# A bias row for two tiles on one engine, and two one-hots in one comparison, in a graph network's edge loop

## The chip, the cores and the metric

The kernel runs on one NeuronCore of a Trainium2 chip. The metric is the device time of one execution in microseconds (us); the times are medians of several runs. The profile and the trace come from one more, profiled execution. "TensorE" is PE in the rows, its weight loads are PEld, VectorE is DVE, ScalarE is ACT, GpSimd is POOL and SyncE is SP.

## The reference, cut to what matters

There are 1250 nodes of 512 features and 20000 edges, sorted by their destination. Two graph layers run one after the other. The first (layer norm, relu, sum over in-edges, two matrix products with batch norm) is not touched. The second is:

```python
h = mish(concat([x[src], x[dst], edge_attr], -1) @ W1 + b1)   # first edge layer, 20000 x 512
messages = mish(h @ W2 + b2)                                  # second edge layer, 20000 x 512
agg = segment_sum(messages, dst, num_segments=1250)
u = mish(concat([x, agg], -1) @ W3 + b3)
out = u @ W4 + b4                                             # then x + out, layer norm, residual
```

with `mish(x) = x * tanh(softplus(x))`. `b2` is one row of 512 values, the same for every edge.

## The kernel before, in words

The products `x @ W1` for the source and the destination part are made once per node and stored as two tables. The edges are cut into tiles of 128, two tiles to a **step** (numbered s, from 0 to 78; step 78 has one tile). Each step gathers its rows of both tables (GpSimd's indirect DMAs), and then five kinds of work run, each engine in its own written order and all tied by semaphores:

- **z1** (TensorE, `z1`, L1099 and L1106): transposes the gathered rows into PSUM and adds the edge attributes' product. It waits for `h_full` of step s-1, since there is one pair of banks `Z1`.
- **mish 1** (ScalarE, `exp1`, `sq1`, `log1`, `inv1`, L1422 to L1434), then VectorE: `full1` (L2098, tile `h_full`, in two halves), `hi1` (L2108, the rounded part of h) and `lo1` (L2112, the rest of h).
- **z2** (TensorE, `z2`): for each of the two tiles k = 0 and 1 of the step, h times W2 in three terms of four matmuls: `h_hi` by both parts of W2 (L1124, L1125), then `h_lo` by one part (L1129). Each is a 128x512 matmul. The result of tile k of step s stands in bank `2 * (s % 2) + k` of `Z2`.
- **mish 2** (ScalarE, `exp2` to `inv2`, L1446 to L1458), then VectorE: `message` (L2123), `hi2` (L2133), `lo2` (L2137).
- **segment** (TensorE, L1149): four matmuls of the one-hot destinations with the messages. VectorE makes the one-hots (`hots1`, L1645, by comparing a row of numbers with each edge's destination). Two steps, an odd and the even one after it, gather in one bank; VectorE adds the bank to the nodes (`add_group`, L1656, two instructions) in every even step of its own order, after it has waited for `seg_done`.

The orders are these. TensorE in step s: z1 of s; z2 of s-2, tile 1; segment of s-4; z2 of s-1, tile 0. VectorE in step s: full1 of s; hi2 of s-3; hi1 of s; lo2 of s-3; message of s-2; one-hots of s-2; b2 row for step s; lo1 of s; in even steps the sums of s-3. ScalarE in step s: exp1, sq1, log1 of s; exp2 of s-2; inv1 of s; sq2; (in odd steps the b2 copy for s-1); log2; inv2 of s-2. A second part of the sums for destinations outside the usual window stands in a branch that is entered only where it is needed.

The bias b2 has to stand in a Z2 bank before the matmuls that accumulate there. From step 2 on three ways are used. For tile 0 VectorE copies the row (`b2_first_tile`, L2127), in every step. For tile 1 of even steps ScalarE copies it (`b2_second_tile`, L1461). For tile 1 of odd steps TensorE makes it by a matmul of ones with the row (L1122), as it does for all four tiles of steps 0 and 1. TensorE waits for a semaphore ahead of a z2 whose row was copied:

```python
if after(s, 2) and k == 0:
    pe.wait_ge(b2_first, s - 1)
elif after(s, 2) and j == 0:
    pe.wait_ge(b2_second, s)
else:
    pe.matmul(at, ONES_R[:, :], B2_R[:, :], start=True, stop=False, ...)
```

Here j is s % 2 and `after(s, 2)` is true from step 2 on. VectorE may write the row only when `message` of step s-2, which reads the same banks, is done.

Of the kernel before, what the change touches and what calls it, by code (L numbers as in the profile page):

```python
# [17 lines left out]
ALU = mybir.AluOpType  # L18
# [8 lines left out]
P = 128  # L27
NODES, DIM, HID0, EDGE_DIM = 1250, 512, 1024, 64
# [95 lines left out]
def gnn_kernel(nc, x, src_cols, dst_cols, dst_rows, edge_attr_t, eps, cols, rows, w01, w02,  # L124
               w1, w2, w3, w4, out):
    ctx = ExitStack()
    with ctx:
# [3 lines left out]
        def sb(name, shape, dt=F32, at=None):  # L131
            size = 2 if dt in (F16, I16) else 4
            for n in shape[1:]:
                size *= n
            if at is None:
                at = place[0]
                place[0] += size + (-size) % 32
            return nc.alloc_sbuf_tensor_at(name, shape, dt, offset=at), at + size + (-size) % 32
# [27 lines left out]
        REL_G, _ = sb("dst_in_group", [P, TILES])  # L166
# [5 lines left out]
        ONEHOT, _ = sb("onehot", [P, 2, 2, P], F32R)  # L172
# [16 lines left out]
        IOTA, _ = sb("iota", [P, NP])  # L189
# [4 lines left out]
        B2_ROW, _ = sb("b2_row", [P, 1, DIM], at=place[0] - 4 * 4 * PW)  # L194
# [132 lines left out]
        def h_high(s, j):  # L327
            return EARLY_HI[:, :, :] if early(s, 1) else H_HI[:, j, :, :]

        def h_low(s, j):  # L330
            return EARLY_LO[:, :, :] if early(s, 1) else H_LO[:, j, :, :]
# [27 lines left out]
        Z1, SEG, Z2 = BANKS[:, 0:2, :], BANKS[:, 2:4, :], BANKS[:, 4:8, :]  # L359
# [13 lines left out]
        def sem(name):  # L373
            return ctx.enter_context(nc.semaphore(name))
# [20 lines left out]
        hot_ready, seg_done, agg_done = sem("hot_ready"), sem("seg_done"), sem("agg_done")  # L395
# [16 lines left out]
        z1_done, a_exp, a_sq, a_ln, a_r, h_hi, h_lo = (sem(n) for n in  # L412
            ("z1_done", "a_exp", "a_sq", "a_ln", "a_r", "h_hi", "h_lo"))
        h_full = [sem(f"h_full_{h}") for h in range(2)]
        z2_done, b2_in, b2_first, b2_second = (sem(n) for n in ("z2_done", "b2_row_in", "b2_in_first_tile", "b2_in_second_tile"))
        b_exp, b_sq, b_ln, b_r, msg_full, msg_hi, msg_lo = (sem(n) for n in
            ("b_exp", "b_sq", "b_ln", "b_r", "msg_full", "msg_hi", "msg_lo"))
        u_bias, u_exp, u_cut, u_sq, u_ln, u_r, u_ready = (sem(n) for n in
# [13 lines left out]
        def live(s):  # L432

            return not isinstance(s, int) or 0 <= s < EDGE_PAIRS

        def tiles(s):

            return min(2, EDGE_TILES - 2 * s) if isinstance(s, int) else 2
# [7 lines left out]
        def after(s, first):  # L446

            return not isinstance(s, int) or s >= first
# [387 lines left out]
        def _(pe):  # L836
# [273 lines left out]
            def z2(s, j, k):  # L1110

                at, e = Z2[:, 2 * j + k, :], slice(k * P, (k + 1) * P)
                if k == 0:
                    if not after(s, 2):
                        pe.wait_ge(up_moved, BLOCKS * KD)
                    pe.wait_ge(h_hi, s + 1)
                if after(s, 2) and k == 0:
                    pe.wait_ge(b2_first, s - 1)
                elif after(s, 2) and j == 0:
                    pe.wait_ge(b2_second, s)  # L1120
                else:
                    pe.matmul(at, ONES_R[:, :], B2_R[:, :], start=True, stop=False, skip_group_check=True)  # L1122
                for c in range(KD):
                    pe.matmul(at, h_high(s, j)[:, c, e], W2_LO[:, c, :], start=False, stop=False, skip_group_check=True)  # L1124
                    pe.matmul(at, h_high(s, j)[:, c, e], W2_HI[:, c, :], start=False, stop=False, skip_group_check=True)  # L1125
                if k == 0:
                    pe.wait_ge(h_lo, s + 1)
                for c in range(KD):
                    mm = pe.matmul(at, h_low(s, j)[:, c, e], W2_HI[:, c, :], start=False, stop=(c == KD - 1), skip_group_check=True)  # L1129
                if k == tiles(s) - 1:  # L1130
                    mm.then_inc(z2_done, 1)
# [43 lines left out]
            for b in range(BLOCKS):  # L1175
                for o in range(KD):
                    n = KD * b + o
# [5 lines left out]
                    if n in Z1_BEHIND:  # L1183
                        s = Z1_BEHIND.index(n)
# [58 lines left out]
        def _(act):  # L1243
# [174 lines left out]
            def exp1(s):  # L1418
                act.wait_ge(z1_done, s + 1)
                if after(s, 1):  # L1420
                    act.wait_ge(h_full[1], s)
                nc.scalar.activation(z1_work(s)[:, :, 0:P * tiles(s)], Z1v[:, :, 0:P * tiles(s)], ACT.Exp).then_inc(a_exp, 1)  # L1422
# [34 lines left out]
                act.wait_ge(b_ln, s + 1)  # L1457
                nc.scalar.activation(z2_work(s), z2_work(s), ACT.Exp, scale=-1.0).then_inc(b_r, 1)  # L1458

            def b2_second_tile(s, j):  # L1460
                nc.scalar.copy(Z2[:, 2 * j + 1, :], B2_ROW[:, 0, :]).then_inc(b2_second, 2)  # L1461

            def edge_step(s, j):

                if live(s):
                    exp1(s)
                    sq1(s)
                    log1(s)
                if live(s - 2):
                    exp2(s - 2, j)  # L1470
                if live(s):
                    inv1(s)
                if live(s - 2):
                    sq2(s - 2)
                if j == 1 and after(s, 3) and live(s - 1) and tiles(s - 1) == 2:
                    b2_second_tile(s - 1, 1 - j)
                if live(s - 2):
                    log2(s - 2)
                if live(s - 2):
                    inv2(s - 2)  # L1480

            act.wait_ge(q_stored, TABLE_STORED)
            for b in range(BLOCKS):
                for o in range(KD):
                    n = KD * b + o
# [4 lines left out]
                    for s, first in enumerate(Z1_BEHIND):  # L1490
# [5 lines left out]
                            log1(s)  # L1496
                        if n == first + 3:
                            inv1(s)
            act.wait_ge(b2_in, 16)
            for s in range(2, 4):  # L1500
                edge_step(s, s % 2)
            with act.Fori(2, LAST - 1) as i:
# [66 lines left out]
        def _(dve):  # L1569
# [61 lines left out]
            def load_range(n, row):  # L1631

                dve.load(range_regs[n][:R_USED], range_words(row, R_LOW, R_USED))
# [8 lines left out]
            def make_hots(hots, rel, tile, past=0):  # L1642

                for j, at in enumerate(hots):
                    ins = nc.vector.tensor_scalar(at, IOTA[:, bass.ds(past * P, P)], rel[:, bass.ds(tile + j, 1)], None, ALU.is_equal)  # L1645
                return ins
# [467 lines left out]

            def hots1(s, j):

                make_hots([ONEHOT[:, j, k, :] for k in range(2)], REL_G, 2 * s).then_inc(hot_ready, 1)

            def message(s, j):
                dve.wait_ge(b_r, s + 1)  # L2120
# [1 line left out]
                    dve.wait_ge(msg_lo, s)  # L2122
                nc.vector.scalar_tensor_tensor(MSG[:, :, :], EB[:, :, :], -0.5, z2_out(s, j), ALU.add, ALU.mult).then_inc(msg_full, 1)  # L2123

            def b2_first_tile(s, j):
                dve.wait_ge(msg_full, s - 1)
                nc.vector.tensor_copy(Z2[:, 2 * j, :], B2_ROW[:, 0, :]).then_inc(b2_first, 1)  # L2127

            def hi2(s):
                dve.wait_ge(msg_full, s + 1)  # L2130
# [27 lines left out]
            def edge_step(s, j, i):  # L2158

                if live(s):  # L2160
                    for h in range(2):
                        full1(s, h)
                if live(s - 3):
                    hi2(s - 3)
                if live(s):
                    hi1(s, j)
                if live(s - 3):
                    lo2(s - 3)
                if live(s - 2):
                    message(s - 2, j)  # L2170
                if live(s - 2):
                    hots1(s - 2, j)
                    if live(s):
                        b2_first_tile(s, j)
                if live(s):
                    lo1(s, j)
                if live(s - 3):
                    sums1(s - 3, i - 2 + j, j == 0)
                if live(s - 2) and j == 0:
                    load_range(0, i - 1)  # L2180
# [159 lines left out]
```

## Time and profile before

| | before |
|---|---|
| time, median of 3 runs (lowest to highest) | 1098.36 us (1097.97 to 1099.22) |
| the profiled execution: its own time | 1101.45 us |
| its span in the trace | 1099.6 us |
| TensorE busy, matmuls / weight loads | 1041.4 us (95%) / 875.5 us (80%) |
| VectorE busy | 869.0 us (79%) |
| ScalarE busy | 886.9 us (81%) |
| GpSimd busy | 716.9 us (65%) |
| granted TensorE clock over the span, mean | 0.977 of full |
| chain that ended last, by engine | TensorE 86%, VectorE 7%, ScalarE 3% |

The span is the profiled stretch from the first to the last instruction. The edge loop takes it from about 370 us to 1032 us. "Busy" counts an engine's instructions and not its register, wait or branch instructions; weight loads run beside matmuls. A matmul of 128x512 shows 0.39 us in its row while the next one starts 0.23 us later, because they are pipelined.

### The profile page before, as it was taken

The page shows a single profiled execution, that of the slowest core. Times are in us where ns is not written, and L with a number is a line of the kernel's source. Part 1 is how long each engine was busy: PE and PEld are TensorE (multiplying, and loading weights), DVE is VectorE, ACT ScalarE, POOL GpSimd, SP SyncE. Part 2 cuts the span into 40 slices and gives each one's busy share as a digit, 9 for nine tenths or more (in the row PEclk, how much of TensorE's full clock was granted, in tenths as well). Part 3 has the DMA queues.
Part 4 walks back from the last instruction along what each step waited for, and adds up shares of the span by engine and source line. Part 5 has one row for each costly group of instructions (what it writes and reads, how often), then busy time and mean ns, then how long its engine had stood idle before and what let it go on. Part 6 is the DMA issues. An engine that isn't in the chain of part 4 may idle for free.

```text
span 1099.6 us, 18587 instructions
## 1 busy us (share of the span) xinstructions
PE 1041.4 (95%) x5641; PEld 875.5 (80%) x5642; DVE 869.0 (79%) x1504; ACT 886.9 (81%) x1081; POOL 716.9 (65%) x622
## 2 busy tenths in 40 slices
PE   3568999999999999999999999999999999999997
PEld 1126889999789888888888888888888888888796
DVE  7898536634525389999999999999999999999786
ACT  6985845523613699999999999999999999999584
POOL 6875448643255487777777777777777777760217
PEclk8769999999999999999999999999999999999999
DMA  3004972674165386676666667666666666661002
GB/s 105 8 1 113 177 230 76 228 252 142 59 229 115 78 198 162 158 165 140 137 140 147 135 140 143 145 138 140 145 139 137 145 143 137 142 127 39 1 1 94
DMA packets 82914, 141.63 MB, mean 129 GB/s; under 512 B 11115, under 2 KB 39020, under 8 KB 82742
## 3 DMA queue, kind: packets, MB, share of 16 engines
q0 software_dynamic: 38048, 87.58, 39.2%
q1 hardware_dynamic: 44822, 53.52, 15.1%
q8 instruction: 21, 0.34, 0.1%
q14 instruction: 23, 0.19, 0.1%
HBM read 115.42 MB, written 20.39 MB: 124 GB/s over the span
## 4 chain that ended last, share of the span: by engine, by line
PE 86%; DVE 7%; ACT 3%; issue 2%; POOL 1%; DMA 1%; DVEq 1%; POOLq 0%; ACTq 0%
PE banks L1124 13%; PE banks L1125 13%; PE banks L1129 13%; PE banks L1023 9%; PE banks L1106 7%; PE banks L1149 7%; PE banks L1099 6%; PE banks L1066 5%; PE banks L941 4%; PE banks L1087 4%; PE banks L1210 2%; DVE edge_counts L1790 2%; DVE key_onehot L1729 1%; PE banks L996 1%; PE banks L871 1%
## 5 line engine op out<-in xcount | busy, mean ns | idle before, releaser
L774 POOL DMA_INDIRECT gather_pq<-q_table,dst x157 | 323.4, 2060 | 57.1 <-issue 47.5
L766 POOL DMA_INDIRECT gather_pq<-p_table,src x157 | 174.7, 1113 | 119.5 <-PE banks L1106 68.5
L1124 PE MATMUL banks<-w_lo,h_hi 128*128 128x512 f32 x620 | 241.9, 390 | 0.0
L1125 PE MATMUL banks<-w_hi,h_hi 128*128 128x512 f32 x620 | 241.7, 390 | 0.0
L1129 PE MATMUL banks<-w_hi,h_lo 128*128 128x512 f32 x620 | 166.0, 390 | 0.0
L1129 PEld LDWEIGHTS banks<-w_hi,h_lo 128*128 128x128 f32 x620 | 116.4, 188 | 24.3
L1125 PEld LDWEIGHTS banks<-w_hi,h_hi 128*128 128x128 f32 x620 | 116.4, 188 | 23.7
L1124 PEld LDWEIGHTS banks<-w_lo,h_hi 128*128 128x128 f32 x620 | 116.4, 188 | 23.3 <-issue 0.6
L2098 DVE SCALAR_TENSOR_TENSOR h_full<-mish_work,banks 128x512 f32<-128x512 f32 (+1 forms) x154 | 98.4, 680 | 44.5 <-ACT mish_work L1434 41.4
L2123 DVE SCALAR_TENSOR_TENSOR message<-mish_work,banks 128x1024 f32<-128x1024 f32 x78 | 95.3, 1222 | 8.4 <-ACT mish_work L1458 0.3
L1099 PE MATMUL banks<-ident,gather_pq 128*128 128x128 f32 x628 | 96.5, 275 | 0.6 <-DVE h_full L2098 0.3
L1106 PE MATMUL banks<-edge_attr_parts,we_hi 128*128 128x256 f32 (+1 forms) x316 | 94.6, 322 | 0.0
L2137 DVE TENSOR_TENSOR message_lo<-message,message_hi 128x1024 fp32r<-128x1024 f32 x78 | 94.3, 1209 | 0.1
L2112 DVE TENSOR_TENSOR h_lo<-h_full,h_hi 128x1024 fp32r<-128x1024 f32 (+1 forms) x77 | 93.1, 1209 | 0.0
L1099 PEld LDWEIGHTS banks<-ident,gather_pq 128*128 128x128 f32 x628 | 72.0, 140 | 17.3 <-DVE h_full L2098 11.0
L1458 ACT ACTIVATE mish_work<-mish_work 128x1024 f32<-128x1024 f32 (+1 forms) x79 | 83.5, 1057 | 2.5
L1454 ACT ACTIVATE mish_work<-mish_work 128x1024 f32<-128x1024 f32 (+1 forms) x79 | 83.2, 1054 | 1.3
L1422 ACT ACTIVATE mish_work<-banks 128x1024 f32<-128x1024 f32 (+1 forms) x77 | 78.6, 1021 | 6.0 <-PE banks L1106 5.2
L1426 ACT ACTIVATE mish_work<-mish_work 128x1024 f32<-128x1024 f32 (+1 forms) x77 | 81.3, 1056 | 2.5
L1430 ACT ACTIVATE mish_work<-mish_work 128x1024 f32<-128x1024 f32 (+1 forms) x77 | 81.3, 1056 | 2.4
L1450 ACT ACTIVATE mish_work<-mish_work 128x1024 f32<-128x1024 f32 (+1 forms) x79 | 82.4, 1043 | 0.1
L1106 PE MATMUL banks<-edge_attr_parts,we_lo 128*128 128x256 f32 (+1 forms) x316 | 81.6, 280 | 0.0
(270 smaller groups left out, 2623.4 us busy)
## 6 DMA issues: line engine op xcount, KB each, us to landing
edge_attr<-in_edge_attr_t SPq DMA_DIRECT2D x20, 256.0 KB, 2.9
attr_high<-edge_attr_hi SPq DMA_DIRECT2D x40, 128.0 KB, 2.1
attr_low<-edge_attr_lo SPq DMA_DIRECT2D x40, 128.0 KB, 1.8
edge_attr_parts<-attr_high SPq DMA_DIRECT2D x79, 64.0 KB, 2.5
edge_attr_parts<-attr_low SPq DMA_DIRECT2D x79, 64.0 KB, 2.4
x_nodes<-h_hi POOLq DMA_DIRECT2D x10, 256.0 KB, 14.9
x_nodes<-h_lo POOLq DMA_DIRECT2D x10, 256.0 KB, 7.8
p_table<-p_stage SPq DMA_DIRECT2D x10, 256.0 KB, 2.0
```

Of the source, the lines that this page charges most:

```text
L766: nc.gpsimd.indirect_dma_start(GP[:, 2 * j + k, :], None, p_tab[:, :], bass.IndirectOffsetOnAxis(ap=SRC[:, 2 * s + k:2 * s + k + 1], axis= ...
L774: nc.gpsimd.indirect_dma_start(GP[:, 2 * j + k, :], None, q_tab[:, :], bass.IndirectOffsetOnAxis(ap=DST[:, 2 * s + k:2 * s + k + 1], axis= ...
L1023: mm = pe.matmul(bank, weights[w][:, k, o * P:(o + 1) * P], acts[a](k)[:, nodes], start=(k == 0 and n == 0), stop=(k == kn - 1 and n == 2) ...
L1099: pe.matmul(Z1v[:, c, k * P:(k + 1) * P], GP[:, 2 * slot + k, c * P:(c + 1) * P], IDENT[:, :], is_transpose=True, skip_group_check=True, s ...
L1106: mm = pe.matmul(Z1v[:, c, 0:P * tiles(s)], w[:, c * P:(c + 1) * P], AT_R[:, slot, 0:P * tiles(s)], skip_group_check=True, start=False, st ...
L1124: pe.matmul(at, h_high(s, j)[:, c, e], W2_LO[:, c, :], start=False, stop=False, skip_group_check=True)
L1125: pe.matmul(at, h_high(s, j)[:, c, e], W2_HI[:, c, :], start=False, stop=False, skip_group_check=True)
L1129: mm = pe.matmul(at, h_low(s, j)[:, c, e], W2_HI[:, c, :], start=False, stop=(c == KD - 1), skip_group_check=True)
L2098: nc.vector.scalar_tensor_tensor(h_full_of(s)[:, at[0], at[1]], z1_work(s)[:, at[0], at[1]], -0.5, Z1v[:, at[0], at[1]], ALU.add, ALU.mult ...
L2112: nc.vector.tensor_tensor(h_low(s, j)[:, :, 0:P * tiles(s)], h_full_of(s)[:, :, 0:P * tiles(s)], h_high(s, j)[:, :, 0:P * tiles(s)].bitcas ...
L2123: nc.vector.scalar_tensor_tensor(MSG[:, :, :], EB[:, :, :], -0.5, z2_out(s, j), ALU.add, ALU.mult).then_inc(msg_full, 1)
L2137: nc.vector.tensor_tensor(MSG_LO[:, :, :], MSG[:, :, :], MSG_HI[:, :, :].bitcast(F32), ALU.subtract).then_inc(msg_lo, 1)
```

## The change

VectorE copies the b2 row into both tiles' banks in every step from 2 on, in one instruction of 1024 columns. ScalarE's copy and its semaphore are gone, and so is TensorE's bias matmul from step 2 on; TensorE waits for the one new semaphore ahead of tile 0 of each step. The two one-hots of a step are made by one tensor-tensor comparison of 256 columns, whose operands are the row of numbers, repeated for both tiles, and each tile's column of destinations, repeated 128 times.

```diff
-                if after(s, 2) and k == 0:
-                    pe.wait_ge(b2_first, s - 1)
-                elif after(s, 2) and j == 0:
-                    pe.wait_ge(b2_second, s)
+                if after(s, 2):
+                    if k == 0:
+                        pe.wait_ge(b2_seeded, s - 1)
                 else:
                     pe.matmul(at, ONES_R[:, :], B2_R[:, :], start=True, stop=False, skip_group_check=True)
...
-            def b2_second_tile(s, j):
-                nc.scalar.copy(Z2[:, 2 * j + 1, :], B2_ROW[:, 0, :]).then_inc(b2_second, 2)
...
-                if j == 1 and after(s, 3) and live(s - 1) and tiles(s - 1) == 2:
-                    b2_second_tile(s - 1, 1 - j)
...
-                make_hots([ONEHOT[:, j, k, :] for k in range(2)], REL_G, 2 * s).then_inc(hot_ready, 1)
+                wide = [P, 2, P]
+                nc.vector.tensor_tensor(ONEHOT[:, j, :, :], IOTA[:, 0:P].rearrange("p (o k) -> p o k", o=1).broadcast_to(wide),
+                                        REL_G[:, bass.ds(2 * s, 2)].rearrange("p (t o) -> p t o", o=1).broadcast_to(wide),
+                                        ALU.is_equal).then_inc(hot_ready, 1)
...
-            def b2_first_tile(s, j):
+            def b2_both_tiles(s, j):
                 dve.wait_ge(msg_full, s - 1)
-                nc.vector.tensor_copy(Z2[:, 2 * j, :], B2_ROW[:, 0, :]).then_inc(b2_first, 1)
+                nc.vector.tensor_copy(Z2[:, 2 * j:2 * j + 2, :], B2_ROW[:, :, :].broadcast_to([P, 2, DIM])).then_inc(b2_seeded, 1)
```

`make_hots` issued one tensor-scalar comparison of 128 columns for each tile. ScalarE's wait for the row's load, ahead of its loop, is also taken out.

## Rows read from the trace of the kernel before

**Rows 1.** Busy time by engine, 400 to 1000 us, granted clock, DMA share, GB/s.
```profile
400.00:1000.00 600.00, 600.00 (x3185) 507.38 (x3185) 550.30 (x790) 591.21 (x611) 455.51 (x281) 1.00 0.67 141
```

**Rows 2.** Instructions of L1122, L1461, L2127: duration min/median/max, first and last start.
```profile
L1122 PE MATMUL banks<-b_parts,ones x42: 389/397/497, 369.7 to 1016.5; 128*128 128x512 f32 x42
...
L1461 ACT COPY banks<-b_row x38: 584/586/592, 388.8 to 1008.0; 128x512 f32<-128x512 f32 x38
...
L2127 DVE COPY banks<-b_row x77: 683/685/691, 384.6 to 1019.2; 128x512 f32<-128x512 f32 x77
```

**Rows 3.** Timeline of VectorE: start us, duration us, instruction [idle before it].
```profile
606.04 1.28 DVE L2098 SCALAR_TENSOR_TENSOR h_full<-mish_work,banks 128x512 f32<-128x512 f32 x2
...
611.29 0.68 DVE L2127 COPY banks<-b_row 128x512 f32<-128x512 f32 x1
611.89 1.21 DVE L2112 TENSOR_TENSOR h_lo<-h_full,h_hi 128x1024 fp32r<-128x1024 f32 x1
613.96 1.28 DVE L2098 SCALAR_TENSOR_TENSOR h_full<-mish_work,banks 128x512 f32<-128x512 f32 x2 [0.85 <-ACT mish_work L1434]
...
618.83 0.48 DVE L1645 TENSOR_SCALAR onehot<-iota,dst_in_group 128x128 fp32r<-128x128 f32 x2
619.22 0.69 DVE L2127 COPY banks<-b_row 128x512 f32<-128x512 f32 x1
619.81 1.22 DVE L2112 TENSOR_TENSOR h_lo<-h_full,h_hi 128x1024 fp32r<-128x1024 f32 x1
621.29 0.75 DVE L1656 SCALAR_TENSOR_TENSOR agg_nodes<-banks,from_low,agg_nodes 128x512 f32 x1 [0.26 <-issue]
621.96 0.74 DVE L1656 SCALAR_TENSOR_TENSOR agg_nodes<-banks,below_low,agg_nodes 128x512 f32 x1
622.78 1.28 DVE L2098 SCALAR_TENSOR_TENSOR h_full<-mish_work,banks 128x512 f32<-128x512 f32 x2
```

**Rows 4.** TensorE and its weight loads: timelines; the L1122 row from the chain.
```profile
606.78 0.31 PEld L1099 LDWEIGHTS banks<-ident,gather_pq 128*128 128x128 f32 x3 [0.28 <-DVE h_full L2098]
...
612.13 0.19 PEld L1124 LDWEIGHTS banks<-w_lo,h_hi 128*128 128x128 f32 x1
...
612.58 0.39 PE L1125 MATMUL banks<-w_hi,h_hi 128*128 128x512 f32 x1
...
617.06 0.23 PE banks L1122
...
620.55 0.39 PE L1149 MATMUL banks<-message_lo,onehot 128*128 128x512 f32 x1
```

**Rows 5.** Timelines of VectorE, the weight loads and TensorE near the loop's end.
```profile
1012.82 0.69 DVE L2127 COPY banks<-b_row 128x512 f32<-128x512 f32 x1
...
1013.62 0.19 PEld L1124 LDWEIGHTS banks<-w_lo,h_hi 128*128 128x128 f32 x1 [0.41 <-issue]
...
1013.96 0.40 PE L1125 MATMUL banks<-w_hi,h_hi 128*128 128x512 f32 x1
```

**Rows 6.** Timelines of TensorE and VectorE where the sums come first.
```profile
402.81 0.39 PE L1149 MATMUL banks<-message_lo,onehot 128*128 128x512 f32 x1
...
402.35 1.21 DVE L2112 TENSOR_TENSOR h_lo<-h_full,h_hi 128x1024 fp32r<-128x1024 f32 x1
403.56 0.75 DVE L1656 SCALAR_TENSOR_TENSOR agg_nodes<-banks,from_low,agg_nodes 128x512 f32 x1
```

**Rows 7.** Groups by line and shape: count | busy us, mean ns | idle before.
```profile
L2123 DVE SCALAR_TENSOR_TENSOR message<-mish_work,banks 128x1024 f32<-128x1024 f32 x78 | 95.3, 1222 | 8.4 <-ACT mish_work L1458 0.3
...
L2133 DVE CAST message_hi<-message 128x1024 fp32r<-128x1024 f32 x78 | 53.9, 690 | 0.4 <-DVE message L2123 0.4
...
L2021 DVE TENSOR_TENSOR x_nodes<-x_nodes,banks 128x256 f32<-128x256 f32 x4 | 1.6, 409 | 1.3 <-PE banks L996 1.3
...
L1981 DVE SCALAR_TENSOR_TENSOR dst_in_group<-ranges,dst_f 128x160 f32<-128x160 f32 x1 | 0.3, 314 | 0.0
...
L1719 DVE SCALAR_TENSOR_TENSOR key<-src_parts,dst_from_lowest 128x160 f32<-128x160 f32 x1 | 0.3, 313 | 0.0
```

More of the change, by code:

```diff
@@ L414, in gnn_kernel @@
         h_full = [sem(f"h_full_{h}") for h in range(2)]
-        z2_done, b2_in, b2_first, b2_second = (sem(n) for n in ("z2_done", "b2_row_in", "b2_in_first_tile", "b2_in_second_tile"))
+        z2_done, b2_in, b2_seeded = (sem(n) for n in ("z2_done", "b2_row_in", "b2_in_both_tiles"))
         b_exp, b_sq, b_ln, b_r, msg_full, msg_hi, msg_lo = (sem(n) for n in
@@ L1474, in edge_step @@
                     sq2(s - 2)
-                if j == 1 and after(s, 3) and live(s - 1) and tiles(s - 1) == 2:
-                    b2_second_tile(s - 1, 1 - j)
-                if live(s - 2):
                     log2(s - 2)
@@ L1498, in _ @@
                             inv1(s)
-            act.wait_ge(b2_in, 16)
             for s in range(2, 4):
@@ L2173, in edge_step @@
                     if live(s):
-                        b2_first_tile(s, j)
+                        b2_both_tiles(s, j)
                 if live(s):
```

## The prediction, made before the changed kernel ran

> **What bounds the kernel now.** The engines' busy time by stage comes first. Between 400 and 1000 us the kernel runs its edge loop; TensorE is busy in every microsecond, ScalarE in 591 of 600 and VectorE in 550, at the full clock [rows 1]. With three engines this full, shares do not say which waits decide, so the timelines of one period come next. A period is two steps (an even pair of tiles, then an odd one). ScalarE's copy runs once in each, 38 times from 388.8 to 1008.0, which makes (1008.0 - 388.8) / 37 = 16.74 us a period [rows 2].
>
> In the period from 606.04 VectorE begins h_full of an odd step at 606.04 and of the next even step at 613.96, after 0.85 us idle for ScalarE's last exponential, and the next odd one at 622.78 [rows 3]. So there is slack of 0.85 us in the odd step's VectorE work. In the even step the only idle is 0.26 us ahead of the node sums (L1656) at 621.29. The profile puts it down to "issue". I read it as a wait for TensorE: the last of the four segment matmuls starts at 620.55 and takes 0.39 [rows 4], so it ends at 620.94 and the sum starts 0.35 later. In the first period that ends in sums the last segment matmul ends at 402.81 + 0.39 = 403.20 and the sum starts at 403.56, 0.36 later, while h_lo before it started 1.21 earlier, against 1.48 at 619.81 [rows 3, 6]. The distance to TensorE is the same and the distance to VectorE's own work is not.
>
> That gives two closed loops.
> - **Loop P:** h_full odd (606.04), TensorE's z1, z2, segment, z2 of the odd pair (first weight load 612.13), z1, the bias matmul, z2, segment (ends 620.94), VectorE's sums, h_full odd (622.78). Length 16.74. TensorE hardly stops in it: the load for z1 at 606.78, which waits for h_full, is the one row in a period with a wait on it [rows 4].
> - **Loop V:** h_full odd, z1, ScalarE's four steps, h_full even: 7.92 us; then VectorE's own chain from h_full even to h_full odd, 8.82 us as measured. Without the wait for the segment it would be shorter: h_lo at 619.81 and, since an instruction here starts about 0.08 before the end of the one ahead, the first sum 1.14 later at 620.95, 0.34 sooner. And the sums' last 0.82 (621.96 to 622.78) would be 0.67, as between the two sums, because the registers would have been loaded meanwhile. So 8.82 - 0.34 - 0.15 = 8.33, and loop V has 0.49 us to spare.
>
> **The change, part by part.**
> *TensorE's bias matmul goes* in odd steps from 3 on. Of 42 such matmuls [rows 2] the four of steps 0 and 1 stay, 38 go. Each holds the chain for 0.23 us [rows 4]. It lies in loop P, between z1 and the segment. Taken alone: -0.23 x 37 = -8.5 us.
> *ScalarE's copy goes*, 38 times 0.59 us. I cost that at nothing: exp of z1 waits for TensorE and h_full even waits for the exponential of that same chain, in which the copy (after the second square) does not stand. VectorE's message waits for ScalarE's last inverse, whose half a microsecond of lead only grows. Its semaphore falls away too.
> *VectorE's row becomes two rows.* The 512-column copy takes 0.69 us [rows 3]. A 1024-column instruction with a PSUM operand takes 1.22 (L2123, mean 1222 ns), so +0.53 for each of 77 copies. The bound below: the 1024-column cast between SBUF tiles takes 0.69 [rows 7], which would make the addition nothing. I take 1.22, since the present copy needs 0.69 for 512 columns: it runs at the rate of the former, with the same fixed part.
> *Two one-hots become one comparison.* Now 0.39 us from the first to the copy (618.83 to 619.22) [rows 3]. One tensor-tensor over 256 columns takes 0.41 (L2021), less 0.08 of overlap, 0.33 [rows 7]: -0.06. Its bounds: 0.27 more if the repeated operands went at half rate, or nothing gained.
> Sum for VectorE: +0.47 us a step, all ahead of h_lo and, for TensorE, ahead of z2.
>
> *The even step.* Its copy would end at 613.96 + 5.26 - 0.06 + 1.22 = 620.38. TensorE reaches that z2 at 620.78 less 0.23, so it waits for nothing. Loop V becomes 7.92 + 8.33 + 0.47 = 16.72: all slack used, no cost, and about 0.02 under today's period.
> *The odd step.* h_full even has 0.85 us of cover, 0.47 of which is used. But TensorE takes the odd z2 sooner here: the copy ends 606.04 + 5.25 - 0.06 + 1.22 = 612.45, after the 612.13 at which its first load starts now [rows 4]. The semaphore wait added here is on TensorE, and the whole of z2, the next z1, z2 and segment are queued behind it. What a late row costs is seen once in the trace, near the end: the copy at 1012.82 ends at 1013.51, the load starts at 1013.62 and the second matmul at 1013.96, 0.45 after the copy's end [rows 5]. So the second matmul would start at 612.90 instead of 612.58: +0.32 in loop P, against -0.23 from the bias matmul. Loop P: 16.74 - 0.23 + 0.32 = 16.83, and it is the longer one. h_lo, also 0.47 later (ends 613.57), is needed only after eight matmuls of 0.23, past 614.4, and stays covered.
>
> So a period grows by 0.08 us (0.02 less to 0.15 more, as the copy or the restart come out 0.05 to 0.1 other than taken). Over the 36 periods between the first sums and the end: +2.9 us. The first period with sums starts its sum when VectorE can, 1.21 after h_lo, so there VectorE's 0.47 shows by about 0.2. In the last three steps VectorE has no pause; three copies of 0.47 come to at most 1.4, less what ScalarE and TensorE hide; I take 0.8. Sum 2.9 + 0.2 + 0.8 = +3.9 us, bounds 0 and 7. On the profiled execution, 1101.45 us (span 1099.6, and 1.85 around it), that is 1105.3. The median shown, 1098.36, lies 3.09 below the profiled one; the same addition gives 1102.2.
>
> **A rule against the change.** The one-hots' second operand repeats one column's value 128 times. In the trace the add of the lowest rows (L1981) reads an operand whose every value is repeated four times, 160 elements, in 314 ns; L1719 reads 160 plain ones twice in 313 ns [rows 7]. Repeating costs nothing there. The Trainium skill ("Vector Engine (DVE) Microarchitecture Reference", section 5.2 on stream behaviour) says that a port streams at the full rate only where elements come in runs of at least two adjacent words, and gives 1.73 ns a column with one source hopping; by that figure the comparison would take an estimated 0.18 us more than I count. The trace speaks against it, in runs of four only; it is the first rival.
>
> **Rivals.**
> *A, slow comparison.* The operand repeated 128 times goes at up to half rate, at most 0.27 us more. The row in PSUM comes later by as much and loop P with it. At two thirds of that bound, 0.18 x 36 = +6.5 on top: 1108.7. For it: no row repeats one value so long. Against: L1981. Chance 0.10.
> *B, faster.* The copy of both rows runs at the pitch of the SBUF casts, 0.69 for 1024 columns. Then the row is in time for TensorE, VectorE's chain is 0.06 shorter, and what is left is the bias matmul's -0.23 a period: 37 x 0.23 = 8.5, 1089.9. It decides once the copy takes under about 0.9, the length at which the load at 612.13 is no longer late. For it: SBUF casts of this size. Against: the copy's own 0.69 for 512 columns. Beside it, the Trainium skill ("VectorE: DVE Perf Modes", "Why PSUM operands drop a tier") holds fp32 with a PSUM operand to one element a cycle; by it B would not occur, and this trace's copy row agrees. Chance 0.13, part of it for a gain that these rows do not show me.
> *C, no slack in the even step.* If the 0.26 ahead of the sums is what the profile calls it, issue time after h_lo [rows 3], VectorE's 0.47 goes into every period in full: 36 x 0.47 + 1 = +18, 1116. Against: the constant 0.35 behind the segment [rows 3, 4, 6]. Chance 0.05.
>
> **How the numbers follow.** The forecast has 0.72, own range 1098 to 1105.5. A run tells 0.2% (2.2 us) from no change, so "same" ends at 1100.6. Of the 0.72 I give 0.22 to the part below that (a period that changes by 0.03 or less) and 0.50 above. Slower: 0.50 + 0.10 + 0.05 = 0.65; same 0.22; faster 0.13. The range 1097.5 to 1108.8 leaves out B, C and little else.
>
> **What would show it.** Period of VectorE's h_full rows: 16.83 (forecast), 16.51 (B), 17.0 (A), 17.2 (C). The copy row 128x1024 at 1.22; the comparison at 0.41. The idle before L1656 gone in even steps, that before h_full even down from 0.85 to about 0.4. On TensorE a new wait once a period at the first load of the odd z2, L1124, put down to the copy; were it missing, loop P is wrong. No L1461 rows, 4 of L1122. ScalarE's idle grows by about 0.6 us a period.

## The result, and the profile after

The changed kernel takes 1103.62 us in the median of its runs (1102.5 to 1105.68), the kernel before 1098.36; the ratio is 1.0046, with a 95% interval of 1.0037 to 1.0054. So it is slower, by 5.1 us (4.1 to 5.9). The prediction said 1102.2, +3.9.

First the page of the kernel after: its span, each engine's busy time, its share and the count of instructions. Behind it, from the same kernel, the busy time by engine from 400 to 1000 us, in the order of [rows 1].

```profile
span 1100.9 us, 18306 instructions
...
PE 1046.8 (95%) x5603; PEld 866.0 (79%) x5604; DVE 901.6 (82%) x1427; ACT 873.9 (79%) x1043; POOL 692.4 (63%) x622
```

```profile
400.00:1000.00 600.00, 597.45 (x3129) 494.02 (x3128) 577.11 (x712) 574.66 (x570) 427.61 (x279) 1.00 0.68 140
```

Against [rows 1] VectorE is busy 26.8 us more and ScalarE 16.5 us less. TensorE, which was busy in every microsecond, now is not for 2.55 us, and it finished 56 matmuls fewer in the same 600 us. About 36 of them are the bias matmuls of some 36 periods; the other 20 it did not get to: it waits.

Next, lines of the kernel after as instructions: duration min/median/max in ns, first and last start in us. They answer to [rows 2]; the last is the first sum of each pair (L1656 before).

```profile
L1121 PE MATMUL banks<-b_parts,ones x4: 389/396/497, 365.8 to 378.7; 128*128 128x512 f32 x4
...
L2122 DVE COPY banks<-b_row x77: 1218/1220/1226, 380.6 to 1020.5; 128x1024 f32<-128x1024 f32 x77
...
L2110 DVE TENSOR_TENSOR onehot<-iota,dst_in_group x77: 416/418/421, 380.3 to 1020.1; 128x256 fp32r<-128x256 f32 x77
...
L1648 DVE SCALAR_TENSOR_TENSOR agg_nodes<-banks,from_low,agg_nodes x40: 742/746/752, 399.9 to 1032.4; 128x512 f32 x40
```

Four bias matmuls are left and no copy by ScalarE. From the first sum to the last it takes 632.5 us here. The same line of the kernel before reads so:

```profile
L1656 DVE SCALAR_TENSOR_TENSOR agg_nodes<-banks,from_low,agg_nodes x40: 743/751/753, 403.6 to 1031.1; 128x512 f32 x40
```

That is 627.5, so the loop became 5.0 us longer. Taken from each odd step's `h_full`, the mean of 36 periods went from 16.736 to 16.868 us (405.07 to 1007.57 before, 401.18 to 1008.43 after): 36 x 0.132 = +4.75. From the last of them to the end it is 92.07 before and 92.47 after, +0.40. The sum, +5.15, agrees with the measured 5.1.

The spans differ by only 1.3 us, because the loop of the profiled execution of before began 3.9 us later. That is no effect of the change: in the profiled runs below, the same point lies anywhere from 400.9 to 405.1, in kernels with the old and with the new loop.

The timeline of VectorE in one period of the kernel after (start us, duration us, instruction [idle before it]), to be read beside [rows 3]:

```profile
603.72 1.28 DVE L2090 SCALAR_TENSOR_TENSOR h_full<-mish_work,banks 128x512 f32<-128x512 f32 x2
...
608.60 0.42 DVE L2110 TENSOR_TENSOR onehot<-iota,dst_in_group 128x256 fp32r<-128x256 f32 x1
608.93 1.22 DVE L2122 COPY banks<-b_row 128x1024 f32<-128x1024 f32 x1
610.06 1.22 DVE L2104 TENSOR_TENSOR h_lo<-h_full,h_hi 128x1024 fp32r<-128x1024 f32 x1
611.65 1.28 DVE L2090 SCALAR_TENSOR_TENSOR h_full<-mish_work,banks 128x512 f32<-128x512 f32 x2 [0.37 <-ACT mish_work L1433]
...
617.98 1.21 DVE L2104 TENSOR_TENSOR h_lo<-h_full,h_hi 128x1024 fp32r<-128x1024 f32 x1
619.11 0.74 DVE L1648 SCALAR_TENSOR_TENSOR agg_nodes<-banks,from_low,agg_nodes 128x512 f32 x1
619.77 0.74 DVE L1648 SCALAR_TENSOR_TENSOR agg_nodes<-banks,below_low,agg_nodes 128x512 f32 x1
620.60 1.28 DVE L2090 SCALAR_TENSOR_TENSOR h_full<-mish_work,banks 128x512 f32<-128x512 f32 x2
```

The idle ahead of the sums (0.26 before) is gone, and the one ahead of the even `h_full` has shrunk from 0.85 to 0.37. TensorE at the odd step's row, in the kernel after, weight loads and matmuls:

```profile
610.27 0.19 PEld L1123 LDWEIGHTS banks<-w_lo,h_hi 128*128 128x128 f32 x1 [0.52 <-issue]
```

```profile
610.30 0.47 PE L1123 MATMUL banks<-w_lo,h_hi 128*128 128x512 f32 x1
610.61 0.40 PE L1124 MATMUL banks<-w_hi,h_hi 128*128 128x512 f32 x1
...
618.37 0.39 PE L1148 MATMUL banks<-message_lo,onehot 128*128 128x512 f32 x1
```

The row's copy ends at 608.93 + 1.22 = 610.15 and the load starts 0.12 later, after a pause that was not there before. The list of waits from 400 to 1000 us of the kernel after (us in total, times, longest) shows it once a period, under two names:

```profile
ACT mish_work L1421 <- PE banks L1106: 13.6, 36, 0.5
DVE h_full L2090 <- ACT mish_work L1433: 13.4, 36, 0.4
PEld banks L1123 <- issue: 10.3, 19, 0.6
PEld banks L1099 <- DVE h_full L2090: 10.0, 35, 0.4
PEld banks L1123 <- DVE banks L2122: 7.6, 17, 0.5
```

19 + 17 = 36. Both names stand for one wait, that for the copy. The distance from the copy's end to the load alternates from period to period, between 0.12, as above, and 0.05. ScalarE now waits for z1 once a period, which it did not before: it has lost its copy, and its work is no longer near the bound.

### The profile page after: what moved, and what is told of

Same layout as the page of the kernel before. It is cut to its first block and busy times, and to the rows that moved or that the text cites. A ratio compares the mean times of both kernels' runs of the same rounds, so it can differ in the third digit from the quotient of the medians.

```text
span 1100.9 us, 18306 instructions
## 1 busy us (share of the span) xinstructions
PE 1046.8 (95%) x5603; PEld 866.0 (79%) x5604; DVE 901.6 (82%) x1427; ACT 873.9 (79%) x1043; POOL 692.4 (63%) x622
## 5 line engine op out<-in xcount | busy, mean ns | idle before, releaser
L774 POOL DMA_INDIRECT gather_pq<-q_table,dst x157 | 297.7, 1896 | 57.4 <-issue 47.5
L1123 PE MATMUL banks<-w_lo,h_hi 128*128 128x512 f32 x620 | 246.2, 397 | 3.5 <-DVE banks L2122 1.9
L2122 DVE COPY banks<-b_row 128x1024 f32<-128x1024 f32 x77 | 94.0, 1221 | 0.0
```

What stands on the lines that cost most here:

```text
L774: nc.gpsimd.indirect_dma_start(GP[:, 2 * j + k, :], None, q_tab[:, :], bass.IndirectOffsetOnAxis(ap=DST[:, 2 * s + k:2 * s + k + 1], axis= ...
L2122: nc.vector.tensor_copy(Z2[:, 2 * j:2 * j + 2, :], B2_ROW[:, :, :].broadcast_to([P, 2, DIM])).then_inc(b2_seeded, 1)
```

## The experiments

The theory, **P**, is the prediction's: the loop through TensorE binds, and the odd row's late copy costs it more than the bias matmul gave back. The rivals are that VectorE's even step binds (C), that the comparison is the culprit (A), and that the matmul's removal was worth nothing. The ratio is always to the kernel before as timed on the same chip, so that kernel's median differs a little from one experiment to another; "period" is the mean from one odd step's `h_full` to the next in the profiled execution, over the same 36 periods in every kernel, 16.736 before and 16.868 after.

### One comparison alone

The kernel before, with nothing but the new comparison:

```diff
-                make_hots([ONEHOT[:, j, k, :] for k in range(2)], REL_G, 2 * s).then_inc(hot_ready, 1)
+                nc.vector.tensor_tensor(ONEHOT[:, j, :, :], ..., ..., ALU.is_equal).then_inc(hot_ready, 1)
```

> The kernel before with the one comparison alone. Theory P: VectorE is not in the binding loop ahead of the segment, so its 0.06 us a step goes into slack: ratio 1.000 (within 0.001). Rival V (VectorE's time counts in every step): 0.12 us a period, 4 us less, ratio 0.996.

1099.91 against 1100.08 us, ratio 1.0001 (0.999 to 1.0012), period 16.744. In even steps the comparison gains VectorE 0.05 us (the copy begins 5.21 instead of 5.26 after the even `h_full`). In odd steps it gains nothing here (5.28, and 5.27 before), because the cast of the messages, which stands ahead of it, takes over 0.73 us in 35 of the 36 odd steps, where 3 did before. The kernel gains nothing. With only about 0.06 a period left to gain, rival V would have come to an estimated ratio of 0.998, which the interval still leaves out. The rival A is out: the comparison costs no time.

### 0.3 us more on VectorE, in the even or in the odd step

A comparison of 184 columns, whose result nobody reads, is added to the kernel before. In the first kernel it stands behind `h_lo` in even steps, in the second ahead of the row's copy in odd ones:

```diff
+            def pad():
+                nc.vector.tensor_tensor(PAD[:, :], IOTA[:, 0:184], IOTA[:, 0:184], ALU.is_equal)
...
                     lo1(s, j)
+                    if live(s - 2) and j == 0:
+                        pad()
```

```diff
                     hots1(s - 2, j)
+                    if j == 1:
+                        pad()
                     if live(s):
                         b2_first_tile(s, j)
```

> The kernel before, with one more VectorE instruction (184 columns, about 0.26 us, its result unused) after h_lo in even steps, just ahead of the idle that the profile calls issue. Reading of the prediction: that idle is a wait for TensorE's segment, the even step has 0.49 us to spare, so nothing changes: period 16.74, ratio 1.000 (within 0.001). Rival C (the idle is issue time and VectorE's chain has no slack there): 37 x 0.26 = 9.6 us more, ratio 1.0088.

> The kernel before, with the same extra instruction (0.26 us) in odd steps, ahead of the copy of the row. Theory P: the row of odd steps, just in time before, comes 0.26 late; the second matmul of that z2 moves from 6.54 to 5.94 + 0.26 + 0.45 = 6.65 after h_full, so the period grows by 0.11 to 0.15: 4 to 5.5 us, ratio 1.0037 to 1.005. Rival (only idle of VectorE itself counts): the odd step has 0.85 us idle, so nothing changes, ratio 1.000.

Even: 1098.16 against 1100.08 us, ratio 0.9988 (0.9977 to 0.9999), period 16.742. VectorE's timeline in that kernel:

```profile
598.89 1.22 DVE L2113 TENSOR_TENSOR h_lo<-h_full,h_hi 128x1024 fp32r<-128x1024 f32 x1
600.03 0.34 DVE L2121 TENSOR_TENSOR pad<-iota 128x184 fp32r<-128x184 f32 x1
600.37 0.75 DVE L1657 SCALAR_TENSOR_TENSOR agg_nodes<-banks,from_low,agg_nodes 128x512 f32 x1
...
601.86 1.29 DVE L2099 SCALAR_TENSOR_TENSOR h_full<-mish_work,banks 128x512 f32<-128x512 f32 x2
```

The pad stands where the idle was, and the time did not rise (the interval ends just under 1.000, and the period is that of before). In TensorE's timeline the last segment matmul ends where it should for that:

```profile
599.63 0.39 PE L1150 MATMUL banks<-message_lo,onehot 128*128 128x512 f32 x1
```

599.63 + 0.39 = 600.02, and the sum follows 0.35 later as before. What the profile calls "issue" there is the wait for the segment. Rival C is out.

Odd: 1105.14 us, ratio 1.0048 (1.0031 to 1.0064), period 16.890. The same third of a microsecond, of which 0.26 goes by before the copy starts, put where VectorE itself still idles afterwards, costs 0.15 a period:

```profile
612.73 0.34 DVE L2121 TENSOR_TENSOR pad<-iota 128x184 fp32r<-128x184 f32 x1
612.99 0.69 DVE L2131 COPY banks<-b_row 128x512 f32<-128x512 f32 x1
...
615.37 1.29 DVE L2099 SCALAR_TENSOR_TENSOR h_full<-mish_work,banks 128x512 f32<-128x512 f32 x2 [0.56 <-ACT mish_work L1435]
```

VectorE still waits 0.56 us for ScalarE. What the pad delays is the row, and by it TensorE: its second matmul of the odd z2 comes 6.66 after the odd `h_full`, where it was 6.54 before. This is P's first half shown in the kernel before, with no second row and no missing matmul. The two pads are one instruction with one price; only the place differs.

### The bias matmul put back

The changed kernel, with TensorE's bias matmul kept for tile 1 of odd steps:

```diff
-                if after(s, 2):
-                    if k == 0:
-                        pe.wait_ge(b2_seeded, s - 1)
-                else:
+                if after(s, 2) and k == 0:
+                    pe.wait_ge(b2_seeded, s - 1)
+                elif not after(s, 2) or j == 1:
                     pe.matmul(at, ONES_R[:, :], B2_R[:, :], start=True, stop=False, ...)
```

> The changed kernel, but TensorE still makes the row of tile 1 in odd steps by its matmul (over VectorE's row). Theory P (the late row stands in TensorE's loop, and the removed matmul had paid for part of it in the same loop): the period of two steps goes from 16.87 to 16.87 + 0.23 = 17.10 us, 8.5 us above the changed kernel, ratio to the kernel before 1.0125. Rival V (in the changed kernel VectorE's own chain sets the period): the matmul lies off that chain, nothing changes against the changed kernel, ratio 1.0046.

1111.71 against 1099.07 us, ratio 1.0112 (1.0087 to 1.0137), period 17.073, +0.205 over the changed kernel. So the matmul was in the loop that binds and its removal is worth 36 x 0.205 = 7.4 us. The change as a whole lost 4.75 in the loop, so everything else in it cost some 12.

### The odd row sooner: three ways

P's own remedy is to bring the odd row in time. First, tile 0's row alone at the old place, and tile 1's behind `h_lo` (even steps as in the changed kernel):

```diff
+                if j == 1:
+                    nc.vector.tensor_copy(Z2[:, 2 * j, :], B2_ROW[:, 0, :]).then_inc(b2_seeded, 1)
+                    return
                 nc.vector.tensor_copy(Z2[:, 2 * j:2 * j + 2, :], B2_ROW[:, :, :].broadcast_to([P, 2, DIM])).then_inc(b2_seeded, 1)
...
                     lo1(s, j)
+                if j == 1 and after(s, 3) and live(s):
+                    b2_odd_second(s, j)
```

> The changed kernel, but in odd steps VectorE writes only tile 0's row at the old place and tile 1's row after h_lo, as a copy of its own (even steps write both at once). ScalarE's copy and TensorE's matmul stay out. Theory P: TensorE's wait for the row in odd steps is gone, its loop falls to 16.74 - 0.23 = 16.51, and VectorE's chain of 7.92 + 8.80 (to 8.85) is the longer one: period 16.72 to 16.77, ratio to before 0.999 to 1.002. Rival V (all of VectorE's added time counts): 0.07 more VectorE work a period than in the changed kernel, 16.94, ratio 1.007.

1102.12 us, ratio 1.0025 (1.0013 to 1.0038), period 16.797. TensorE's wait at the odd row is gone (second matmul 6.57 after the odd `h_full` in the mean, instead of 6.86). The loop through VectorE's even step now binds, as computed: it measures 8.79 from `h_full` even to odd in the median, and in about every second period 16.70 to 16.73 in all. Most of the others are 16.84 or longer, which was not expected; the last section comes back to it.

Second, the copy ahead of the comparison in odd steps:

```diff
                 if live(s - 2):
+                    if j == 1 and live(s):
+                        b2_both_tiles(s, j)
                     hots1(s - 2, j)
-                    if live(s):
+                    if j == 0 and live(s):
                         b2_both_tiles(s, j)
```

> The changed kernel, but in odd steps VectorE copies the row ahead of the comparison. The copy then waits only for message, so it starts about 0.15 us sooner (5.05 after h_full odd instead of 5.20). Theory P: the period falls by as much as the row comes sooner, 16.87 to 16.72, where VectorE's chain (7.92 + 8.80) takes over; period 16.72 to 16.80, ratio to before 1.000 to 1.003. Rival V: VectorE's work is the same, period 16.87, ratio 1.0046 or a little more.

1115.24 us, ratio 1.0125 (1.0097 to 1.0153), period 17.214: a plain miss of every theory. The row did come sooner (the copy ends 6.21 after the odd `h_full` instead of 6.43), and the kernel became slower.

Third, with TensorE's matmul still replaced but ScalarE's copy kept: the kernel before, with the one comparison, and VectorE's second copy only in odd steps, behind `h_lo`.

```diff
+                elif after(s, 2):
+                    pe.wait_ge(b2_odd, s - 1)
                 else:
                     pe.matmul(at, ONES_R[:, :], B2_R[:, :], start=True, stop=False, ...)
...
                     lo1(s, j)
+                if j == 1 and after(s, 3) and live(s):
+                    b2_odd_second(s, j)
```

> The kernel before, with ScalarE's copy for tile 1 of even steps and VectorE's 512-column copy for tile 0 as they were, the one comparison, and only TensorE's matmul replaced: VectorE copies tile 1's row of odd steps after h_lo. Theory P: TensorE's loop falls to 16.51, VectorE's even chain keeps its half microsecond of slack, and its odd step keeps 0.85 + 0.06 - 0.60 = 0.3; ScalarE, whose idle is about 0.14 a period before, becomes the bound at about 16.60: 37 x 0.14 = 5 us under the kernel before, ratio 0.9955. Rival V: VectorE has 0.48 us more work a period than before and the time rises, ratio above 1.005.

1092.88 us, ratio 0.9941 (0.9919 to 0.9962), period 16.580. This beats both kernels. VectorE's timeline of its odd step:

```profile
607.02 0.69 DVE L2132 COPY banks<-b_row 128x512 f32<-128x512 f32 x1
607.62 1.22 DVE L2114 TENSOR_TENSOR h_lo<-h_full,h_hi 128x1024 fp32r<-128x1024 f32 x1
608.75 0.69 DVE L2135 COPY banks<-b_row 128x512 f32<-128x512 f32 x1
609.69 0.69 DVE L2100 SCALAR_TENSOR_TENSOR h_full<-mish_work,banks 128x512 f32<-128x512 f32 x1 [0.25 <-ACT mish_work L1436]
```

The first row is where it was, the second fills the idle ahead of the even `h_full`, and 0.25 of that idle is left in this period (0.25 to 0.51 over the loop). The even step holds nothing new. So the gain of the matmul can be had; the changed kernel gave it back, with more, for a row in the odd step that is late and a row in the even step that ScalarE had been writing for nothing.

### Both rows with the two old comparisons

> The changed kernel with the two old comparisons, so the rows alone. Theory P: the row comes 0.05 us later than in the changed kernel, and the period grows by that: 16.92, 2 us above the changed kernel, ratio to before 1.0065. If only VectorE's chain counted (rival V), the same 0.05 stands in one chain of the even step: 16.92 as well; this run is for the size, that of one comparison's worth where the row is late.

The changed kernel, with `make_hots` as before. 1128.11 against 1100.08 us, ratio 1.0257 (1.0237 to 1.0277), period 17.545 (17.58 without the last two periods, the figure in the expectation below), where +0.05 on the changed kernel had been expected and it was +0.68. This is the second miss, and it shows in VectorE's and GpSimd's timelines of this kernel:

```profile
611.93 0.74 DVE L1648 SCALAR_TENSOR_TENSOR agg_nodes<-banks,from_low,agg_nodes 128x512 f32 x1
612.46 1.56 POOL L774 DMA_INDIRECT gather_pq<-q_table,dst  x1 [0.30 <-issue]
612.59 0.73 DVE L1648 SCALAR_TENSOR_TENSOR agg_nodes<-banks,below_low,agg_nodes 128x512 f32 x1
613.95 1.29 DVE L2090 SCALAR_TENSOR_TENSOR h_full<-mish_work,banks 128x512 f32<-128x512 f32 x2 [0.62 <-issue]
```

Between the second sum and `h_full` VectorE stands still for 0.62 us, and ScalarE has nothing to do with it. What stands in that place of VectorE's order is `load_range`: its sequencer loads three words from SBUF into registers, for the next sums. The line of that load (DVEq, VectorE's sequencer; min/median/max in ns), in the kernel before, in the changed one, in this one, and in the one with the row first:

```profile
L1633 DVEq TENSOR_LOAD <-tile_range x40: 744/750/769, 384.3 to 1029.7; - x40
```

```profile
L1625 DVEq TENSOR_LOAD <-tile_range x40: 744/750/757, 380.4 to 1031.2; - x40
```

```profile
L1625 DVEq TENSOR_LOAD <-tile_range x40: 745/1474/1591, 382.5 to 1057.7; - x40
```

```profile
L1625 DVEq TENSOR_LOAD <-tile_range x40: 745/1380/1583, 384.6 to 1047.7; - x40
```

The load takes 0.75 us in the first two and up to 1.59 in the others. In the kernel with the old comparisons each load of the loop that is long (33 of 35, 1.14 to 1.59 us) has one of GpSimd's gathers from the second table (L774) begin 0.14 to 0.17 us after its own start; above, the load starts at 612.29 and the gather at 612.46. With the row first it is 0.13 to 0.35 us in 34 of 35. In the kernels before and after, no gather begins in the load's first 0.5 us. This made a theory, **L**: a register load is stretched when a gather begins early in it, and VectorE's sums had been moved onto such a place. It was tried by moving the load.

### The register load moved

In these kernels `load_range` is issued in the odd step behind `h_lo`, where VectorE waits for ScalarE anyway:

```diff
                     lo1(s, j)
+                if live(s - 2) and j == 1:
+                    load_range(0, i - 1)
                 if live(s - 3):
                     sums1(s - 3, i - 2 + j, j == 0)
-                if live(s - 2) and j == 0:
+                if isinstance(s, int) and s == FINAL:
                     load_range(0, i - 1)
```

First with the two old comparisons:

> The run of the rows alone, whose period was 17.58 and not 16.92, with one move: VectorE's register load of the next group's ranges, which its sequencer makes behind the node sums of even steps, is issued in the odd step instead, behind h_lo. Theory L (the missed 0.66 us is that load, 1.48 long where a GpSimd gather of the second table begins inside it, and 0.75 elsewhere): the h_full of odd steps comes about 0.65 us after the second sum again, the period is 16.92 - 0.17 = 16.75 (to 16.85), ratio to before 1.000 to 1.006. Rival (the old pair of comparisons with the long copy costs it in another way): 17.4 or more, ratio above 1.02.

Then with the row first in odd steps:

> The run with the row ahead of the comparison in odd steps, with the same move of the load. Theory L with P: its load too was 1.44 long. Without it TensorE's loop is 16.87 - 0.22 (row sooner) - 0.17 (load) = 16.5 and VectorE's chain 7.92 + 8.80 = 16.72 is the bound: 16.70 to 16.80, ratio 0.999 to 1.003. Rival (the order of copy and comparison itself cost the time): stays near 17.2, ratio 1.0125.

The two come to 1104.12 (ratio 1.0046, 1.0033 to 1.0059; period 16.856) and 1100.95 us (ratio 1.0019, 1.0009 to 1.0028; period 16.780) against 1098.86. The first came down from 1.0257, the second from 1.0125, each by nothing but this move. The load's line, in the one and in the other:

```profile
L1625 DVEq TENSOR_LOAD <-tile_range x40: 744/751/760, 391.5 to 1033.1; - x40
```

```profile
L1625 DVEq TENSOR_LOAD <-tile_range x40: 743/749/764, 391.5 to 1030.3; - x40
```

Both came out at the ratios that were expected, the first with its period at the upper end (16.856, where 16.85 was the limit), and the rivals, 1.02 and 1.0125, are out. The kernel with the row first is now faster than the changed kernel, as P had said of it: with both rows by VectorE and the odd one sooner (TensorE's second matmul at 6.67 instead of 6.86) it makes 16.78, near the 16.72 of VectorE's own loop.

The changed kernel with the load moved, and the best one (the row split, ScalarE's copy kept) with it:

> The changed kernel with the same move of the load, which is not stretched there. Theory P: the load's 0.17 us stands in TensorE's loop behind the segment (h_full comes 1.84 after it, 1.67 without), so the period falls from 16.87 to about 16.72, where VectorE's chain ends it: 5 us under the changed kernel, ratio to before 1.000 (0.998 to 1.002). Rival (VectorE has idle in the loop, a load in its sequencer costs nothing): 16.87, ratio 1.0046.

> The fastest run so far (only TensorE's matmul replaced, by a VectorE copy behind h_lo; period 16.58) with the same move of the load. TensorE's loop falls from 16.51 to 16.35, and ScalarE, at about 16.6 a period, stays the bound: period 16.50 to 16.58, ratio to before 0.9935 to 0.995. If TensorE's loop was the bound there: 16.42, ratio 0.990.

The changed kernel: 1102.43 us, ratio 1.0031 (1.0019 to 1.0042), period 16.821 and not 16.72, a miss; the interval overlaps that of the changed kernel. `h_full` odd does follow the segment's end sooner (1.72 in the mean and 1.67 in the median, instead of 1.83), but the late row comes 0.07 later still, which took most of it back. The casts of the messages are the groups that differ, first in the changed kernel and then in this one (count | busy us, mean ns | idle before):

```profile
L2128 DVE CAST message_hi<-message 128x1024 fp32r<-128x1024 f32 x78 | 54.3, 697 | 0.0
```

```profile
L2128 DVE CAST message_hi<-message 128x1024 fp32r<-128x1024 f32 x78 | 58.1, 745 | 0.0
```

34 of the loop's 72 take over 0.73 us, where 4 did, and the 28 of them in odd steps stand ahead of the late row. Why they do was not settled: gathers run beside the slow ones and beside the fast ones.

The best one: 1092.27 us, ratio 0.9931 (0.9918 to 0.9943), period 16.564. The intervals of the two versions of it overlap, so the moved load is not shown to help there. In its busy times by engine from 400 to 1000 us, TensorE (first number behind the 600.00 of the stretch) never stands, and ScalarE (fourth of them) is idle for 8 us of 600. Its periods alternate between about 16.37 and 16.76, and which wait makes them do so was not looked into:

```profile
400.00:1000.00 600.00, 600.00 (x3186) 505.73 (x3184) 575.98 (x763) 592.00 (x617) 453.12 (x281) 1.00 0.68 143
```

## Why the prediction was right, and where its sizes were off

**What binds.** Loop P was named as the bound, with VectorE's 0.26 us of "issue" ahead of the sums read as a wait for the segment. The even pad took that idle away and cost nothing, and the odd pad cost 0.15. Loop P it is, before and after: in both kernels `h_full` odd starts 1.84 us after the last segment matmul's end.

**TensorE's matmul.** Given as -0.23 a period. Put back, it cost +0.205.

**ScalarE's copy.** Costed at nothing. ScalarE is busy 16.5 us less in 600, 0.47 a period where the prediction said about 0.6, and waits for TensorE instead. No run removed this copy alone. What its removal did cost is the row that VectorE has to write in its place. Two of the kernels differ in little but that: with the odd row split in both, the period is 16.58 where ScalarE writes the even row and 16.80 where VectorE does, with 8.26 to 8.58 from `h_full` even to odd in the one and 8.79 (median) in the other. The prediction had that chain at 8.33 + 0.47 = 8.80, and as free only because loop P was longer.

**VectorE's row.** Given as 1.22 us, it took 1.220. Rival B, which needed 0.69, is out. The rate is that of the 512-column copy.

**The comparison.** Given as 0.41 us, it took 0.418, and 0.33 up to the next instruction. An operand whose one value is repeated 128 times goes at the full rate. The Trainium skill ("Vector Engine (DVE) Microarchitecture Reference", section 5.2 on stream behaviour) asks for runs of two adjacent words; the trace does not bear that out for an operand that does not move at all, since by the skill's 1.73 ns a column the instruction would have taken an estimated 0.60, the measured 0.418 and the 0.18 that the prediction worked out from that figure.

**The late row.** It was put at 6.41 us after the odd `h_full` (copy's end) and 6.86 (second matmul); it came at 6.42 to 6.48 and, in turn, at about 6.82 and 6.89, 6.86 in the mean. The wait stands at the load that was named, once a period.

**The period.** Here the size was off: +0.13 us and not +0.08 (bounds 0.02 less to 0.15 more). The prediction's sum was 6.86 to the second matmul, 8.13 from there to the segment's end ([rows 4], less the bias matmul) and 1.84 back to `h_full`. Measured are 6.86, 8.175 and 1.83 in the mean. So the missing 0.04 lies in the second term. Some 0.03 of it is on TensorE just behind its restart: the ten pitches (from one matmul's start to the next) after the second matmul add up to 2.300 us there, and to 2.267 in the kernel with the odd row behind `h_lo`, where TensorE does not stop. The sum let it go at full pace from the second matmul on. Over 36 periods the 0.04 make 1.5 us. A slip of 0.01 comes on top: the prediction's own terms, 16.74 - 0.23 + 0.32, make +0.09, and it went on with 0.08.

**The ends.** The first period and the tail were given +0.2 and +0.8. The tail took +0.40; the first period can't be told, since the loop's start moves by 4 us between executions. Of +3.9 forecast, +2.9 should have been in the loop and +4.75 was.

**Rival C**, no slack in the even step, would have made the period 17.2. It is out. But the way to such a period was open, by a mechanism that no rival named: with 0.06 us more of VectorE work in each step than the changed kernel has, the period was 17.55, because the sums fell onto the gathers. That the forecast held is in part the luck of where its sums fell.

## What to carry to other kernels

When several engines are nearly full, follow one value round through all of them until it comes back; a third of a microsecond in that loop costs at every turn, and the same third beside it costs nothing, whatever the busy shares say. Work moved from an engine with a full share to one with a smaller share helps only if its result is in time for who takes it: ask at which moment each bank is taken, and split the work so that only the part needed first stands in front. And a step that moves by a few hundredths can meet something that it did not meet before: when a result misses by more than its terms allow, look at register loads and other sequencer work, which no busy time shows.

## What the runs showed of the hardware that was not expected

**A register load can take twice as long beside a gather.** VectorE's three words from SBUF take 0.75 us and up to 1.59 when an indirect DMA of GpSimd begins within 0.35 us after the load's start. Over all these kernels' loops there are 504 such loads. In 53 a gather begins 0.1 to 0.2 us after the load's start, and they take 1.49 in the median (0.80 to 1.59); in 23 it is 0.2 to 0.3 (median 1.08), in 25 it is 0.3 to 0.4 (0.95). Of the other 403 two are long (1.48 and 1.57; a gather had begun 0.41 and 0.13 before them) and the rest take 0.74 to 0.78, also where a gather had begun 0.3 before. The Trainium skill ("DMA: Bandwidth & Descriptors", the section on latency and other measured facts) gives such a load a floor of about 600 ns. The trace has the three words above it, at 0.75. TensorE's load of one word lies below it, at 0.30, and it too grows, up to 1.0; its line in the kernel with the old comparisons:

```profile
L843 PEldq TENSOR_LOAD <-tile_range x79: 295/301/1005, 385.5 to 1056.0; - x79
```

In the kernel with the odd second row behind `h_lo` this load and VectorE's (0.75 to 1.11 us, median 0.955 where a gather begins in it) are both long in part. TensorE's takes 0.70 to 0.95 us in every second period, where a gather has begun 0.5 to 0.6 before the load's start, and 0.30 to 0.49 in the others, where one begins 0.1 or less before it. The long ones are, in the main, the periods of 16.84 and more: z1's first weight load, which the register load stands ahead of, mostly starts 0.16 to 0.24 after the end of `h_full`'s first half there, and 0.05 after it in the others. The same stands in the two kernels of the first pair with VectorE's load moved, where z1 starts up to 0.3 late in every second period and `h_full` odd to even takes 7.99 in the mean instead of 7.93; that is part of why they came out above 16.75. Moving VectorE's load removed its own stretch and not TensorE's. The way from the gather to the load was not looked into: a shared port and a shared path would look the same here.

**A restart of TensorE costs more than its pause.** In the changed kernel the load follows the copy's end by 0.05 or 0.12 us, in turn, and the second matmul by 0.39 or 0.45, so that it is 0.31 or 0.34 behind the first, where the pitch is 0.227 otherwise. The next 3 to 11 pitches (4 in the commonest case) are 0.224 to 0.240. All of this is at a granted clock of 1.00, the level of 2.4 GHz.
